# Half of the streamed weight loads issued from GpSimd instead of SyncE, and the last three phases in blocks of their own, in a transformer layer on 8 cores

## The chip, the cores and the metric

The kernel runs on the 8 cores of one Trainium2 chip. The sequence of 8192 tokens is split: each core computes 1024 output rows and recomputes what it needs of the 1024 rows before them, so no core waits for another. Every core reads the weights whole. The metric is the device time in microseconds (us) of the slowest core.

## The reference

```python
x = x + attn(layernorm(x))          # x: (1, 8192, 2048)
x = x + ffn(layernorm(x))
# attn: qkv = h @ Wqkv; q, k = rmsnorm over 2048; 16 heads of 128; rope;
#       scores where 0 <= q_idx - k_idx <= 1023; softmax; o @ Wo
# ffn:  x_q = 0.5 * sign of x beyond +-0.33, else 0
#       w = (0.6 * sign of weight beyond +-0.2, else 0) + rram_variation
#       y = einsum('bsd,od->bso', x_q, w)
```

All weights are float32 in HBM: Wqkv is 2048 x 6144, Wo, weight and rram_variation are 2048 x 2048. The products are made in bfloat16.

## The kernel before, in words

The program is written out by hand. A `Plan` collects one list of instructions per engine. Each engine works through its own list in order; waits on semaphores are entries of the same list, so whatever stands behind a wait on an engine waits too. The DMAs are issued by two engines: SyncE (SP) issues the loads of activations and weights, GpSimd (POOL) the other transfers. `Plan.run` (lines 127 to 134) writes the lists out as a block; at the end of a block all engines meet.

The blocks, by the names in the code:

- P0 and P1 load constants and normalize the core's 16 tiles of 128 rows; xlnT holds them transposed.
- P2k, P3q and P4v are the three projections. Each calls `qkv_pass` (line 360) for 4 chunks of 512 output columns. A chunk is first built: for d = 0 to 15, a 128 x 512 float32 piece of the weight (256 KB) is loaded into a staging buffer, wstgA for even d and wstgB for odd d (called A and B here), and VectorE (DVE) casts it into `wchunk` (line 383). Load d + 2 waits for the cast of piece d, since it overwrites the same staging buffer (line 378). Then TensorE (PE) waits for the last cast (line 386) and multiplies all 16 pieces for each row tile (line 394; 16 row tiles for k and v, 8 for q); ScalarE (ACT) moves each result out of PSUM (line 403). DVE begins the next chunk's casts when the last matmul of this chunk is done (line 373). There is only one `wchunk`, so PE has nothing to do while a chunk is built.
- In P4v, each evacuated v tile is spilled to HBM by a DMA of POOL (vhbm, lines 526 to 531), 16 spills per chunk.
- P5attn is the attention. It loads no weights.
- The last block, P8ffn, holds three phases. Output projection (lines 682 to 732): 128 transposes of the attention output, then 4 chunks of Wo, built as above with casts on line 705, matmuls on line 720 and the residual add on line 727. The residual piece of x_all comes by a DMA of POOL, one for each row tile and chunk, 4 buffers deep (lines 711 to 714). The first chunk is built while PE still transposes. Second layernorm and quantization (lines 737 to 785). FFN (lines 788 to 850): 4 chunks, and for each piece two loads, W (wfT) and R (rrT). ACT applies Sign to W twice (lines 811, 813), DVE adds the two (line 817) and then combines them with R into `wchunk` (line 822). There are two slots of buffers: slot 0 is wstgA and wstgB, slot 1 the two halves of ropeo. The loads of a slot wait for line 822 of its last use. After the build come the matmuls (line 835), the last sum on DVE (line 843), and the store of y by POOL, 8 per chunk (line 848).

Where the next chunk's first loads have a free buffer, SP issues them while PE still multiplies the chunk before.

```python
            for d in range(16):
                si = d % 2
                stg = wstgA if si == 0 else wstgB
                if stg_guard[si] is not None:
                    pl.wait("sync", cv, stg_guard[si])
                ld = pl.dma("sync", stg[:], ..., WS[si])
                pl.wait("vector", WS[si], ld)
```

Of the kernel before, what the change touches and what calls it, by code (L numbers as in the profile page):

```python
# [136 lines left out]
def build_nc(kphases=99, p1lvl=4):  # L137
    nc = bass.Bass("TRN2", target_bir_lowering=False)
# [3 lines left out]
    wo_d = nc.dram_tensor("wo", [D, D], F32, kind="ExternalInput").ap()  # L142
    wfT_d = nc.dram_tensor("wfT", [D, D], F32, kind="ExternalInput").ap()
    rrT_d = nc.dram_tensor("rrT", [D, D], F32, kind="ExternalInput").ap()
# [75 lines left out]
    WS = [Ctr(nc, "wA"), Ctr(nc, "wB"), Ctr(nc, "wC"), Ctr(nc, "wD")]  # L220
    dC = Ctr(nc, "dC")
    SP = [Ctr(nc, "spA"), Ctr(nc, "spB")]
    RNG = Ctr(nc, "rng")
    XR = [Ctr(nc, "xr0"), Ctr(nc, "xr1"), Ctr(nc, "xr2"), Ctr(nc, "xr3")]
    dO = Ctr(nc, "dO")
    ct = Ctr(nc, "ct")
    cv = Ctr(nc, "cv")
    cs = Ctr(nc, "cs")
    OWN = {"vector": cv, "scalar": cs}
# [25 lines left out]
    p = Plan(nc, OWN)  # L255
# [44 lines left out]
    p = Plan(nc, OWN)  # L300
# [59 lines left out]
    def qkv_pass(pl, col0, nchunks, tiles, dst_fn, pre_evac=None, post_evac=None,  # L360
                 w_dram=None, lhs_col=None):
        if w_dram is None:
            w_dram = wqkv_d
        if lhs_col is None:
            lhs_col = lambda t, d: 128 * (16 * t + d)
        ev = {}
        stg_guard = [None, None]
        par_guard = [None, None]
        prev_mm = None
        for ci in range(nchunks):  # L370
            c0 = col0 + 512 * ci
            if prev_mm is not None:
                pl.wait("vector", ct, prev_mm)
            for d in range(16):
                si = d % 2
                stg = wstgA if si == 0 else wstgB
                if stg_guard[si] is not None:
                    pl.wait("sync", cv, stg_guard[si])
                ld = pl.dma("sync", stg[:], w_dram[128 * d:128 * (d + 1), c0:c0 + 512],
                            WS[si])  # L380
                pl.wait("vector", WS[si], ld)
                dstw = wchunk[:, 512 * d:512 * (d + 1)]
                stg_guard[si] = pl.op("vector", lambda e, s=stg, w=dstw: e.tensor_copy(  # L383
                    out=w, in_=s), ins=[stg[:]], out=dstw, sem=cv)
            cast15 = stg_guard[1]
            pl.wait("tensor", cv, cast15)
            for ti, t in enumerate(tiles):
                par = ti % 2
                ps = (psA if par == 0 else psB)[:, 0:512]
                if par_guard[par] is not None:  # L390
                    pl.wait("tensor", cs, par_guard[par])
                ctm = None
                for d in range(16):
                    ctm = pl.op("tensor", lambda e, d=d, t=t, ps=ps: e.matmul(  # L394
                        ps, xlnT[:, lhs_col(t, d):lhs_col(t, d) + 128],
                        wchunk[:, 512 * d:512 * (d + 1)],
                        start=(d == 0), stop=(d == 15)),
                        sem=(ct if d == 15 else None))
                pl.wait("scalar", ct, ctm)
                if pre_evac is not None:  # L400
                    pre_evac(pl, t, ci)
                dst = dst_fn(t, ci)
                ev[(t, ci)] = pl.op("scalar", lambda e, ps=ps, dd=dst: e.copy(dd, ps),  # L403
                                    ins=[ps], out=dst, sem=cs)
                par_guard[par] = ev[(t, ci)]
                if post_evac is not None:
                    post_evac(pl, t, ci, ev[(t, ci)])
            prev_mm = ctm
        return ev
# [77 lines left out]
    p = Plan(nc, OWN)  # L487
# [12 lines left out]
    p = Plan(nc, OWN)  # L500
# [192 lines left out]
    for ci in range(4):  # L693
        c0 = 512 * ci
        if prev_mm6 is not None:
            p.wait("vector", ct, prev_mm6)
        for d in range(16):
            si = d % 2
            stg = wstgA if si == 0 else wstgB
            if stg_guard6[si] is not None:  # L700
                p.wait("sync", cv, stg_guard6[si])
            ld = p.dma("sync", stg[:], wo_d[128 * d:128 * (d + 1), c0:c0 + 512], WS[si])
            p.wait("vector", WS[si], ld)
            dstw = wchunk[:, 512 * d:512 * (d + 1)]
            stg_guard6[si] = p.op("vector", lambda e, s=stg, w=dstw: e.tensor_copy(  # L705
                out=w, in_=s), ins=[stg[:]], out=dstw, sem=cv)
        p.wait("tensor", cv, stg_guard6[1])
        for j in range(NQ):
            si = j % 4
            ps = (psA if j % 2 == 0 else psB)[:, 0:512]  # L710
            if xres_guard[si] is not None:
                p.wait("gpsimd", cv, xres_guard[si])
            xl = p.dma("gpsimd", xres[:, 512 * si:512 * (si + 1)],
                       x_d[128 * (8 + j):128 * (9 + j), c0:c0 + 512], XR[si])
            if par_guard6[j % 2] is not None:
                p.wait("tensor", cv, par_guard6[j % 2])
            ctm = None
            for h in range(NH):
                c0o = o_sb_base + 2048 * j + 128 * h
                ctm = p.op("tensor", lambda e, ps=ps, c0o=c0o, h=h: e.matmul(  # L720
                    ps, R1[:, c0o:c0o + 128], wchunk[:, 512 * h:512 * (h + 1)],
                    start=(h == 0), stop=(h == NH - 1)),
                    sem=(ct if h == NH - 1 else None))
            p.wait("vector", ct, ctm)
            p.wait("vector", XR[si], xl)
            dstx = x2[:, 2048 * j + c0:2048 * j + c0 + 512]
            evj = p.op("vector", lambda e, ps=ps, si=si, dd=dstx: e.tensor_add(
                dd, ps, xres[:, 512 * si:512 * (si + 1)]),
                ins=[ps, xres[:, 512 * si:512 * (si + 1)]], out=dstx, sem=cv)
            xres_guard[si] = evj  # L730
            par_guard6[j % 2] = evj
        prev_mm6 = ctm

    x2done = cv.v
    p.wait("scalar", cv, x2done)
    p.wait("vector", cv, x2done)
    th_of = lambda j: thr[:, 2 * j:2 * j + 1]
    tl_of = lambda j: thr[:, 2 * j + 1:2 * j + 2]
    tr7 = tr6
    cvx_prev = None  # L740
    for j in range(NQ):
        xt = x2[:, 2048 * j:2048 * (j + 1)]
# [40 lines left out]
            c0 = 2048 * j + 128 * d  # L783
            tr7.do(p, xqT[:, c0:c0 + 128], xqT[:, c0:c0 + 128], scale=0.5)
    cs_xqT = cs.v
    cvx_last = cvx_prev

    tmpA = [PTb[:, 0:512], PTb[:, 1024:1536]]
    tmpB = [PTb[:, 512:1024], PTb[:, 1536:2048]]
    stgW = [wstgA, ro2stgA[:, 0:512]]  # L790
    stgR = [wstgB, ro2stgA[:, 512:1024]]
    out_guard = None
    built_guard = [stg_guard6[1], max(stg_guard6[1] or 0, cvx_last or 0)]
    p.wait("scalar", cv, cvx_last)
    par_guard8 = [par_guard6[0], par_guard6[1]]
    prev_mm8 = None
    for ci in range(4):
        c0 = 512 * ci
# [1 line left out]
            p.wait("vector", ct, prev_mm8)  # L800
        for d in range(16):
            si = d % 2
            if built_guard[si] is not None:
                p.wait("sync", cv, built_guard[si])
                p.wait("scalar", cv, built_guard[si])
            ldw = p.dma("sync", stgW[si][:], wfT_d[128 * d:128 * (d + 1), c0:c0 + 512],
                        WS[si])
            ldr = p.dma("sync", stgR[si][:], rrT_d[128 * d:128 * (d + 1), c0:c0 + 512],
                        WS[2 + si])
            p.wait("scalar", WS[si], ldw)  # L810
            p.op("scalar", lambda e, s=stgW[si], tA=tmpA[si]: e.activation(  # L811
                out=tA, in_=s[:], func=AF.Sign, bias=-0.2), ins=[stgW[si][:]], out=tmpA[si])
            sgn = p.op("scalar", lambda e, s=stgW[si], tB=tmpB[si]: e.activation(  # L813
                out=tB, in_=s[:], func=AF.Sign, bias=0.2), ins=[stgW[si][:]], out=tmpB[si],
                sem=cs)
            p.wait("vector", cs, sgn)
            p.op("vector", lambda e, tA=tmpA[si], tB=tmpB[si]: e.tensor_add(tA, tA, tB),
                 ins=[tmpA[si], tmpB[si]], out=tmpA[si])
            p.wait("vector", WS[2 + si], ldr)
            dstw = wchunk[:, 512 * d:512 * (d + 1)]  # L820
            built_guard[si] = p.op(
                "vector", lambda e, s=stgR[si], w=dstw, tA=tmpA[si]: e.scalar_tensor_tensor(  # L822
                    w, s[:], 3.3333333, tA, ALU.mult, ALU.add),
                ins=[stgR[si][:], tmpA[si]], out=dstw, sem=cv)
# [23 lines left out]
            out_guard = p.dma("gpsimd", y_d[128 * j:128 * (j + 1), c0:c0 + 512],  # L848
                              outstg[:, 0:512], dO)
        prev_mm8 = ctm  # L850
    for cc in [dO, RNG, dC, SP[0], SP[1]] + XR:
        p.streams["gpsimd"].append(lambda e, s=cc.sem, v=cc.v: e.wait_ge(s, v))
    for cc in WS:
        p.streams["sync"].append(lambda e, s=cc.sem, v=cc.v: e.wait_ge(s, v))
# [54 lines left out]
```

## Time and profile before

| what | value |
|---|---|
| time, median of 2 runs | 3243.77 us (3237.33 to 3250.21) |
| profiled execution, its own time | 3240.53 us |
| its span on core 0, the slowest | 3238.5 us |
| spans of the 8 cores | 3218.8 to 3238.5 us |
| PE, ACT, DVE, POOL busy (share of the span) | 57%, 27%, 20%, 2% |
| P2k | about 270 to 884 us |
| P3q | about 884 to 1250 us |
| P4v | about 1250 to 1595 us |
| P5attn | about 1595 to 2502 us |
| output projection | about 2502 to 2767 us |
| second layernorm and quantization | about 2767 to 2903 us |
| FFN | about 2903 us to the end |

All times in the trace are microseconds from the span's start on core 0. The span leaves out 2.0 us of the execution's own time. A row of the timeline gives start, duration, engine, line and operation, and in square brackets how long the engine had been idle and what ended that. SPq is the queue of SyncE. Every DMA is issued from line 118, so loads are told apart by their buffers: wstgB<-wqkv is a load of Wqkv into buffer B.

### The profile page before, as it was taken

How to read it: one execution, taken by the hardware profiler on the slowest of the kernel's cores; microseconds unless marked ns; L12 is line 12 of the kernel's file. 1: busy time of each engine (PE TensorE's matmuls, PEld its weight loads, DVE VectorE, ACT ScalarE, POOL GpSimd, SP SyncE). 2: the span in 40 equal slices, each digit the busy share in tenths (PEclk: the TensorE clock that was granted, in tenths of full speed). 3: DMA queues.
4: the chain of work that ended last, by engine and by line, in shares of the span. 5: the costliest groups of instructions: out<-in, count | busy, mean ns of one | idle time of the engine just before them, and what ended most of it. 6: DMA issues, size and time to landing. Idle time of an engine off the chain costs nothing. (4 is left out here: it accounts for less than half of the span.)

```text
span 3238.5 us, 30548 instructions; the slowest of 8 cores (3218.8 to 3238.5 us)
## 1 busy us (share of the span) xinstructions
PE 1860.4 (57%) x9600; PEld 886.8 (27%) x9600; DVE 643.6 (20%) x1300; ACT 861.6 (27%) x1694; POOL 80.3 (2%) x153
## 2 busy tenths in 40 slices
PE   1223666503336423666898898889889735323333
PEld 0111322201112101232354454445445312101111
DVE  0001000033310032000203312330331121222222
ACT  4672111543301242111122222222123300442221
POOL 0000000000000000010100000000000000000000
PEclk9999888855568755888855555555555667656666
DMA  3211111000031102222200000000000233004333
GB/s 105 76 68 59 52 52 46 0 0 1 13 98 52 46 1 64 77 77 71 83 1 7 7 7 1 7 7 1 7 7 25 75 116 100 4 24 132 127 128 102
DMA packets 72828, 156.23 MB, mean 48 GB/s; under 512 B 12992, under 2 KB 12992, under 8 KB 70368
## 3 DMA queue, kind: packets, MB, share of 16 engines
q1 hardware_dynamic: 62016, 120.61, 11.6%
q0 software_dynamic: 10656, 33.67, 2.9%
q8 instruction: 81, 1.33, 0.2%
q14 instruction: 75, 0.61, 0.1%
HBM read 137.47 MB, written 16.78 MB: 48 GB/s over the span
## 5 line engine op out<-in xcount | busy, mean ns | idle before, releaser
L394 PE MATMUL psA<-wchunk,R 128*128 128x512 bf16 x1280 | 316.6, 404 | 326.8 <-DVE wchunk L383 326.8
L242 PE MATMUL psD<-identb,ropeo 128*128 128x128 bf16 x320 | 84.3, 264 | 488.0 <-DVE ropeo L478 254.8
L394 PE MATMUL psB<-wchunk,R 128*128 128x512 bf16 x1280 | 289.3, 379 | 0.0
L394 PEld LDWEIGHTS psA<-wchunk,R 128*128 128x128 bf16 x1280 | 130.7, 103 | 500.7 <-issue 368.2
L835 PE MATMUL psA<-wchunk,R 128*128 128x512 bf16 x256 | 65.5, 414 | 204.1 <-DVE wchunk L822 204.1
L242 PEld LDWEIGHTS psD<-identb,ropeo 128*128 128x128 bf16 x320 | 33.6, 105 | 539.6 <-issue 539.6
L615 PE MATMUL psA<-R 128*128 128x128 bf16 x576 | 163.5, 284 | 9.9 <-ACT wstgB L595 9.9
L383 DVE CAST wchunk<-wstgA 128x512 bf16<-128x512 f32 x96 | 41.0, 427 | 634.1 <-PE psB L394 439.6
L394 PEld LDWEIGHTS psB<-wchunk,R 128*128 128x128 bf16 x1280 | 125.3, 98 | 151.0
L615 PE MATMUL psB<-R 128*128 128x128 bf16 x576 | 163.7, 284 | 0.0
L246 ACT COPY R<-psD 128x128 bf16<-128x128 bf16 x384 | 101.8, 265 | 216.5 <-PE psC L242 123.6
L649 PE MATMUL psC<-R,PTb 128*128 128x128 bf16 x1152 | 145.6, 311 | 12.5 <-ACT R L666 12.5
L633 DVE TENSOR_TENSOR PTb<-PTb,masksb 128x128 bf16<-128x128 bf16 x128 | 28.8, 225 | 609.3 <-ACT PTb L628 609.3
L628 ACT ACTIVATE PTb<-psA 128x1152 bf16<-128x1152 f32 x64 | 72.3, 1130 | 183.3 <-PE psA L620 183.3
L649 PEld LDWEIGHTS psC<-R,PTb 128*128 128x128 bf16 x1152 | 112.1, 141 | 26.9 <-issue 12.9
L720 PE MATMUL psA<-wchunk,R 128*128 128x512 bf16 x256 | 66.4, 419 | 89.8 <-DVE wchunk L705 89.2
L628 ACT ACTIVATE PTb<-psB 128x1152 bf16<-128x1152 f32 x64 | 72.3, 1130 | 168.6 <-PE psB L620 168.6
L246 ACT COPY R<-psC 128x128 bf16<-128x128 bf16 x384 | 101.8, 265 | 37.8 <-PE psC L242 4.7
L403 ACT CAST R<-psA 128x512 bf16<-128x512 f32 x48 | 28.1, 585 | 305.4 <-PE psA L394 305.4
L573 DVE TENSOR_REDUCE nmaxs<-psA 128x1 f32<-128x1152 f32 x64 | 86.9, 1357 | 78.0 <-PE psA L569 72.2
L242 PE MATMUL psC<-identb,ropeo 128*128 128x128 bf16 x320 | 84.6, 264 | 27.2 <-ACT R L246 4.1
L242 PE MATMUL psD<-identb,R 128*128 128x128 bf16 x128 | 33.9, 265 | 113.8 <-DVE R L778 85.0
(112 smaller groups left out, 2268.6 us busy)
## 6 DMA issues: line engine op xcount, KB each, us to landing
wstgA<-wqkv SPq DMA_DIRECT2D x96, 256.0 KB, 2.7
wstgB<-wqkv SPq DMA_DIRECT2D x96, 256.0 KB, 2.8
wchunk<-x_all SPq DMA_DIRECT2D x16, 1024.0 KB, 4.7
vhbm<-PTb POOLq DMA_DIRECT2D x64, 128.0 KB, 2.1
R<-vhbm POOLq DMA_DIRECT2D x16, 512.0 KB, 4.1
wstgA<-wo SPq DMA_DIRECT2D x32, 256.0 KB, 2.9
wstgB<-wo SPq DMA_DIRECT2D x32, 256.0 KB, 3.0
R<-x_all POOLq DMA_DIRECT2D x32, 256.0 KB, 2.9
```

Of the source, the lines that this page charges most:

```text
L242: tv = pl.op("tensor", lambda e, s=slot, x=src_ap: e.transpose(s, x, identb[:]), sem=ct)
L246: g = pl.op("scalar", lambda e, s=slot, dd=dst_ap: e.copy(dd, s), ins=[slot], out=dst_ap, sem=cs)
L383: stg_guard[si] = pl.op("vector", lambda e, s=stg, w=dstw: e.tensor_copy(out=w, in_=s), ins=[stg[:]], out=dstw, sem=cv)
L394: ctm = pl.op("tensor", lambda e, d=d, t=t, ps=ps: e.matmul(ps, xlnT[:, lhs_col(t, d):lhs_col(t, d) + 128], wchunk[:, 512 * d:512 * (d + 1 ...
L403: ev[(t, ci)] = pl.op("scalar", lambda e, ps=ps, dd=dst: e.copy(dd, ps), ins=[ps], out=dst, sem=cs)
L573: red[h] = p.op("vector", lambda e, ps=ps, h=h: e.tensor_reduce(out=nmaxs[:, h:h + 1], in_=ps[:, 0:1152], axis=AX.X, op=ALU.max, negate=Tr ...
L615: p.op("tensor", lambda e, ps=ps, l=l, kb=kbase, q=q_ap: e.matmul(ps[:, 128 * l:128 * (l + 1)], kT[:, kb + 128 * l:kb + 128 * (l + 1)], q, ...
L628: expv = p.op("scalar", lambda e, ps=ps, PT=PT: e.activation(out=PT, in_=ps[:, 0:1152], func=AF.Exp), ins=[ps[:, 0:1152]], out=PT, sem=cs)
L633: p.op("vector", lambda e, PT=PT: e.tensor_mul(PT[:, 0:128], PT[:, 0:128], masks[:, 0:128]), ins=[PT[:, 0:128]], out=PT[:, 0:128])
L649: p.op("tensor", lambda e, PT=PT, l=l, sl=sl, h=h: e.matmul(psC[:, 0:128], PT[:, 128 * l:128 * (l + 1)], vring[:, 2048 * sl + 128 * h:2048 ...
L720: ctm = p.op("tensor", lambda e, ps=ps, c0o=c0o, h=h: e.matmul(ps, R1[:, c0o:c0o + 128], wchunk[:, 512 * h:512 * (h + 1)], start=(h == 0), ...
L835: ctm = p.op("tensor", lambda e, ps=ps, c0x=c0x, d=d: e.matmul(ps, xqT[:, c0x:c0x + 128], wchunk[:, 512 * d:512 * (d + 1)], start=(d == 0) ...
```

## The change

The pieces of odd d are loaded by POOL, on a new semaphore, instead of by SP, in `qkv_pass` and in the output projection. In the FFN every R load goes to POOL, in both slots, and POOL gets the wait for the slot. The last block is cut in three: P6wo, P7ln2 and P8ffn, each in a Plan of its own. So all engines meet at two more places, and no load of the FFN is issued before the second layernorm's block has ended. The waits that ordered the phases inside the one block are gone.

```diff
@@ qkv_pass
+                qeng = "sync" if si == 0 else "gpsimd"
+                qsem = WS[0] if si == 0 else WG0
                 if stg_guard[si] is not None:
-                    pl.wait("sync", cv, stg_guard[si])
-                ld = pl.dma("sync", stg[:], w_dram[128 * d:128 * (d + 1), c0:c0 + 512],
-                            WS[si])
-                pl.wait("vector", WS[si], ld)
+                    pl.wait(qeng, cv, stg_guard[si])
+                ld = pl.dma(qeng, stg[:], w_dram[128 * d:128 * (d + 1), c0:c0 + 512],
+                            qsem)
+                pl.wait("vector", qsem, ld)
@@ output projection
+            qeng = "sync" if si == 0 else "gpsimd"
+            qsem = WS[0] if si == 0 else WG0
             if stg_guard6[si] is not None:
-                p.wait("sync", cv, stg_guard6[si])
-            ld = p.dma("sync", stg[:], wo_d[128 * d:128 * (d + 1), c0:c0 + 512], WS[si])
-            p.wait("vector", WS[si], ld)
+                p.wait(qeng, cv, stg_guard6[si])
+            ld = p.dma(qeng, stg[:], wo_d[128 * d:128 * (d + 1), c0:c0 + 512], qsem)
+            p.wait("vector", qsem, ld)
@@ before the second layernorm
-    x2done = cv.v
-    p.wait("scalar", cv, x2done)
-    p.wait("vector", cv, x2done)
+    p.run("P6wo")
...
+    p = Plan(nc, OWN)
-    tr7 = tr6
+    tr7 = TrPipe()
@@ before the FFN
-    cvx_last = cvx_prev
-
+    p.run("P7ln2")
...
+    p = Plan(nc, OWN)
-    built_guard = [stg_guard6[1], max(stg_guard6[1] or 0, cvx_last or 0)]
-    p.wait("scalar", cv, cvx_last)
-    par_guard8 = [par_guard6[0], par_guard6[1]]
+    built_guard = [None, None]
+    par_guard8 = [None, None]
@@ FFN
+            rsem = WG0 if si == 0 else WG1
             if built_guard[si] is not None:
                 p.wait("sync", cv, built_guard[si])
+                p.wait("gpsimd", cv, built_guard[si])
                 p.wait("scalar", cv, built_guard[si])
-            ldr = p.dma("sync", stgR[si][:], rrT_d[128 * d:128 * (d + 1), c0:c0 + 512],
-                        WS[2 + si])
+            ldr = p.dma("gpsimd", stgR[si][:], rrT_d[128 * d:128 * (d + 1), c0:c0 + 512],
+                        rsem)
-            p.wait("vector", WS[2 + si], ldr)
+            p.wait("vector", rsem, ldr)
```

POOL's list around P4v, before (the rows of the spills, and the start of P5attn behind them):

```order
L134 UNCONDITIONAL_BRANCH [waits barrier_Pool_Activation_PE_DVE_SP_gather]
L118 DMA vhbm<-PTb 128x512 [waits cs] x64
L130 UNCONDITIONAL_BRANCH
L134 UNCONDITIONAL_BRANCH [waits barrier_Pool_Activation_PE_DVE_SP_gather]
L118 DMA R<-vhbm 128x2048 [waits spA,spB]
```

and the same place now:

```order
L118 DMA wstgB<-wqkv 128x512
L118 DMA wstgB<-wqkv 128x512 [waits cv] x7
L118 DMA vhbm<-PTb 128x512 [waits cs] x16
L118 DMA wstgB<-wqkv 128x512 [waits cv] x8
L118 DMA vhbm<-PTb 128x512 [waits cs] x16
L118 DMA wstgB<-wqkv 128x512 [waits cv] x8
L118 DMA vhbm<-PTb 128x512 [waits cs] x16
L118 DMA wstgB<-wqkv 128x512 [waits cv] x8
L118 DMA vhbm<-PTb 128x512 [waits cs] x16
```

The first B load of chunks 1 to 3 now stands behind the 16 spills of the chunk before.

POOL's list at the end of the program, before (residual loads, stores of y, and the waits of the end):

```order
L130 UNCONDITIONAL_BRANCH
L134 UNCONDITIONAL_BRANCH [waits barrier_Pool_Activation_PE_DVE_SP_gather]
L118 DMA R<-x_all 128x512 x4
L118 DMA R<-x_all 128x512 [waits cv] x28
L118 DMA y<-sa 128x512 [waits cv] x32
L130 UNCONDITIONAL_BRANCH [waits dO,rng,dC,spA,spB,xr0,xr1,xr2,xr3]
```

and now, from the end of the FFN's first build into its second:

```order
L118 DMA wstgB<-rrT 128x512 [waits cv]
L118 DMA ropeo<-rrT 128x512 [waits cv]
L118 DMA y<-sa 128x512 [waits cv] x8
L118 DMA wstgB<-rrT 128x512 [waits cv]
L118 DMA ropeo<-rrT 128x512 [waits cv]
L118 DMA wstgB<-rrT 128x512 [waits cv]
```

The first R loads of chunks 1 to 3 now stand behind the 8 stores of the chunk before.

SP's list inside an FFN build, before (two slots, W and R of each):

```order
L118 DMA wstgA<-wfT 128x512 [waits cv]
L118 DMA wstgB<-rrT 128x512
L118 DMA ropeo<-wfT 128x512 [waits cv]
L118 DMA ropeo<-rrT 128x512
L118 DMA wstgA<-wfT 128x512 [waits cv]
L118 DMA wstgB<-rrT 128x512
```

and now, from the start of its block:

```order
L134 UNCONDITIONAL_BRANCH [waits barrier_Pool_Activation_PE_DVE_SP_release]
L118 DMA wstgA<-wfT 128x512
L118 DMA ropeo<-wfT 128x512
L118 DMA wstgA<-wfT 128x512 [waits cv]
L118 DMA ropeo<-wfT 128x512 [waits cv]
L118 DMA wstgA<-wfT 128x512 [waits cv]
```

SP keeps the W loads alone, and the first two of them stand behind a meeting of all engines.

## Rows read from the trace of the kernel before

**Rows 1.** Waits, whole span: engine line <- waited for: us in total, times, longest.
```profile
PE psA L394 <- DVE wchunk L383: 326.8, 12, 30.4
DVE wchunk L383 <- DMA wstgA<-wqkv: 194.5, 87, 12.5
PE psA L835 <- DVE wchunk L822: 204.1, 4, 52.0
PE psA L720 <- DVE wchunk L705: 89.2, 3, 32.0
```

**Rows 2.** Timeline, K stage, one round: start, us, engine line, [idle before <-releaser].
```profile
533.44 0.43 DVE L383 CAST wchunk<-wstgA 128x512 bf16<-128x512 f32 x1 [2.60 <-DMA wstgA<-wqkv]
533.94 0.33 SPq L118 DMA_DIRECT2D wstgA<-wqkv  x1
534.08 0.43 DVE L383 CAST wchunk<-wstgB 128x512 bf16<-128x512 f32 x1 [0.21 <-DMA wstgB<-wqkv]
```

**Rows 3.** Timeline, K stage, first and last B cast of chunk 0.
```profile
274.39 0.43 DVE L383 CAST wchunk<-wstgB 128x512 bf16<-128x512 f32 x1 [0.28 <-DMA wstgB<-wqkv]
299.41 0.43 DVE L383 CAST wchunk<-wstgB 128x512 bf16<-128x512 f32 x1 [1.63 <-DMA wstgB<-wqkv]
```

**Rows 4.** DMA issues, 270 to 580 us: queue, count, size, median us to landing.
```profile
wstgA<-wqkv SPq DMA_DIRECT2D x32, 256.0 KB, 2.7
wstgB<-wqkv SPq DMA_DIRECT2D x32, 256.0 KB, 2.9
```

**Rows 5.** x_all loads from POOL, 2560 to 2760 us, all 28 of them.
```profile
L118 POOL DMA_DIRECT2D R<-x_all x28: 536/536/545, 2564.5 to 2753.4; - x28
DMA to landing us min/median/max: 2.8/2.9/4.3
```

**Rows 6.** Timeline, output projection: release of a POOL load, and its start.
```profile
2621.00 0.69 DVE L727 TENSOR_TENSOR R<-psA,R 128x512 f32<-128x512 f32 x1 [6.88 <-PE psA L720]
2622.25 0.54 POOL L118 DMA_DIRECT2D R<-x_all  x1 [33.01 <-DVE R L727]
```

**Rows 7.** Timeline, output projection, start of chunk 1's build.
```profile
2588.70 0.54 POOL L118 DMA_DIRECT2D R<-x_all  x1 [2.92 <-DVE wchunk L705]
2589.08 0.33 SPq L118 DMA_DIRECT2D wstgB<-wo  x1
2593.06 0.43 DVE L705 CAST wchunk<-wstgB 128x512 bf16<-128x512 f32 x1 [1.07 <-DMA wstgB<-wo]
```

**Rows 8.** Timeline, V stage, chunk 0 to chunk 1.
```profile
1336.42 0.43 DVE L383 CAST wchunk<-wstgB 128x512 bf16<-128x512 f32 x1
1336.97 0.54 POOL L118 DMA_DIRECT2D vhbm<-PTb  x1 [2.91 <-ACT PTb L403]
```

**Rows 9.** Timeline, FFN, chunk 0 to chunk 1.
```profile
2985.75 0.69 DVE L822 SCALAR_TENSOR_TENSOR wchunk<-wstgB,PTb 128x512 bf16<-128x512 f32 x1
2985.83 0.54 POOL L118 DMA_DIRECT2D y<-sa  x1 [3.22 <-DVE PTb L817]
```

**Rows 10.** Timeline, FFN: issue of an R load, and the step that reads it.
```profile
2912.79 0.43 SPq L118 DMA_DIRECT2D wstgB<-rrT  x1
...
2917.89 0.69 DVE L822 SCALAR_TENSOR_TENSOR wchunk<-wstgB,PTb 128x512 bf16<-128x512 f32 x1
```

**Rows 11.** DMA issues, whole span: W loads of the FFN, slots 0 and 1.
```profile
wstgA<-wfT SPq DMA_DIRECT2D x32, 256.0 KB, 3.0
ropeo<-wfT SPq DMA_DIRECT2D x32, 256.0 KB, 3.3
```

**Rows 12.** Timeline: the join of P1 and P2k.
```profile
270.26 0.27 ACT L246 COPY R<-psC 128x128 bf16<-128x128 bf16 x1 [0.15 <-PE psC L242]
270.78 0.33 SPq L118 DMA_DIRECT2D wstgA<-wqkv  x1
```

**Rows 13.** Timeline, PE: first two output tiles after a build.
```profile
299.98 6.53 PE L394 MATMUL psA<-wchunk,R 128*128 128x512 bf16 x16 [29.87 <-DVE wchunk L383]
306.34 3.62 PE L394 MATMUL psB<-wchunk,R 128*128 128x512 bf16 x16
```

More of the change, by code:

```diff
@@ L225, in build_nc @@
     dO = Ctr(nc, "dO")
+    WG0 = Ctr(nc, "wG0")
+    WG1 = Ctr(nc, "wG1")
     ct = Ctr(nc, "ct")
@@ L732, in build_nc @@
         prev_mm6 = ctm
-    x2done = cv.v
-    p.wait("scalar", cv, x2done)
-    p.wait("vector", cv, x2done)
+    p.run("P6wo")
+    if kphases < 7:
+        return _finish_early()
+    p = Plan(nc, OWN)
     th_of = lambda j: thr[:, 2 * j:2 * j + 1]
     tl_of = lambda j: thr[:, 2 * j + 1:2 * j + 2]
-    tr7 = tr6
+    tr7 = TrPipe()
     cvx_prev = None
@@ L785, in build_nc @@
     cs_xqT = cs.v
-    cvx_last = cvx_prev
+    p.run("P7ln2")
+    if kphases < 8:
+        return _finish_early()
+    p = Plan(nc, OWN)
     tmpA = [PTb[:, 0:512], PTb[:, 1024:1536]]
@@ L850, in build_nc @@
         prev_mm8 = ctm
-    for cc in [dO, RNG, dC, SP[0], SP[1]] + XR:
+    for cc in [dO, RNG, dC, SP[0], SP[1], WG0, WG1] + XR:
         p.streams["gpsimd"].append(lambda e, s=cc.sem, v=cc.v: e.wait_ge(s, v))
```

## The prediction, made before the changed kernel ran

> **What bounds the kernel now.** I read the waits of the whole span first. No engine is full: PE is busy for 57% of the span. PE's largest waits on this change's code are for the last cast of a chunk: 326.8 us in 12 waits in the three projections, 89.2 us in 3 waits in the output projection (its first chunk is built beside the transposes), 204.1 us in 4 waits in the FFN [rows 1]. So 15 builds by casts and 4 FFN builds lie bare on the path that sets the end, and a microsecond more in any of them is a microsecond more in the span.
>
> Next I asked what paces a build. DVE needs 0.43 us for a cast and then stands still for the next load: 2.60 us before the A cast of a round [rows 2], 194.5 us in 87 waits for A alone [rows 1]. The two buffers form two rings of dependence: cast, issue, landing, cast. SP issues 0.07 us after the cast ends (533.44 + 0.43 to 533.94) [rows 2]; the median landing counts from the start of the issue and is 2.7 us for A, 2.9 us for B [rows 4]. From the first to the last B cast of a chunk pass 299.41 - 274.39 = 25.02 us in 7 rounds, 3.57 us each [rows 3]. Check: 0.43 + 0.07 + 2.9 leaves 0.17 us from landing to cast. DVE takes A and B strictly in turn, so the slower buffer paces both. SP is busy for 0.33 us of issue per load [rows 2]: two of them in 3.57 us, so its issuing is not what fills the round.
>
> **The change, part 1: odd loads on POOL, 15 bare builds.** What must be known is the round trip of B through POOL. The trace has the same transfer from POOL, 256 KB of x_all with 128 rows of 2 KB. The release of one ends at 2621.00 + 0.69 = 2621.69 and POOL's instruction starts at 2622.25, 0.56 us later [rows 6], against SP's 0.07. From its start it lands in 2.8 us at least, 2.9 in the median, 4.3 at most, over 28 of them [rows 5]. So the start alone costs 0.49 us a round. For the landing the ends are these. Below: 2.8, 0.1 less than B has now, so +0.39 us. Above: 3.6, halfway between POOL's median and its maximum, so +1.19 us. I take 3.05, near the median with 0.15 on top, because x_all's loads mostly run alone, while B shares the engines with A. When B is slow, A waits for its turn, its cast follows B's at once and A's next load starts together with B's: two transfers from two queues. Three at once show what sharing can cost: POOL at 2588.70 and SP just before it with A, and the B load issued at 2589.08 is cast only at 2593.06, 3.98 us later instead of about 3.1 [rows 7]. My value is a round of 3.57 + 0.49 + 0.15 = 4.21 us. 15 builds of 7 rounds are 105 rounds: 105 x 0.64 = +67 us, ends +41 and +125.
>
> The Trainium skill, page "DMA: Bandwidth & Descriptors", section "Issuing engines are not separate DMA queues", says that all issuing engines share the same DMA engines and that issuing from several saves only the sequencer's time to initiate. The trace agrees in that SP's issue is short beside the landing. The same page (section "Latency and other measured facts") gives a first byte after about 1 us for a POOL load and 0.6 us for an SP load; an estimate by that is +0.4 us a round, +42 us for this part, where the rows give +67.
>
> **Part 2: B loads behind POOL's other work.** In V, the spill of the last row tile starts at 1336.97, while the first B cast of the next chunk runs at 1336.42, from a load that SP had issued long before [rows 8]. Now that load stands behind the spill: start 1336.97 + 0.54 = 1337.51, + 2.9 + 0.17 = 1340.6, so 4.2 us late. Three chunks follow another: +12.5 us (ends +12 and +13). In K and Q, POOL has nothing else, and the first loads stay hidden under the matmuls. In the output projection the residual loads in front wait only for tiles four back, so the first B loads stay hidden too; the first four residual loads of a chunk come behind the build's last B load and have 6.5 us of the first output tile [rows 13] besides; no cost. There is a small gain: they no longer collide with the start of the build, 0.9 us in [rows 7]. For 3 chunks I take -2 us (ends -3 and 0).
>
> In the FFN the first R load of a chunk stands behind the eighth store. The store starts at 2985.83 and the step that needs R ran at 2985.75 [rows 9]. Now: 2985.83 + 0.54 + 2.9 + 0.17 = 2989.4, 3.7 us late, and the slots' next loads wait for that step. Three chunks: +11 us (ends +10 and +12).
>
> **Part 3: R on POOL inside the FFN builds.** R is issued at 2912.79 and used at 2917.89, 5.1 us later [rows 10]. POOL would start it 0.56 us after the slot is free; SP does so after its 0.07 and W's issue of 0.33 us, so the start moves by about 0.2 us. With a landing of 3.6 us it is hidden, more than 1 us to spare. What sets the round there is W: landing, two Signs, two DVE steps. W's landings are 3.0 and 3.3 us in the slots [rows 11], against A's 2.7. Without R in SP's queue they may fall to 2.7-3.0; with R beside them from another queue they may rise by half a microsecond, as B did in [rows 7]. 4 builds of 7 rounds: 28 x (-0.3 to +0.5) = -8 to +14; I take +0.1, +3 us, since the bytes are the same.
>
> **Part 4: blocks of their own.** A meeting of all engines costs little: 270.26 + 0.27 = 270.53 to SP's next issue at 270.78, 0.25 us [rows 12]. Two new ones: 0.5 us. But the FFN's first loads can't be issued in P7 any more: 2.9 + 0.17 us bare. Together +3.6 us (ends +3 and +5). The removed waits were met long before and give nothing.
>
> PE's pace: the first output tile after a build takes 6.53 us and the next 3.62 [rows 13]. That price is paid at each build already, after 29.87 us without matmuls, and I see no reason for it to grow at 34 us.
>
> **Sum**, on the profiled execution's own 3240.5 us: 67 + 12.5 - 2 + 11 + 3 + 3.6 = +95, so 3336. The median of the runs shown is 3.3 us higher, so I forecast 3339 us, 2.9% slower. Adding all low ends gives 41 + 12 - 3 + 10 - 8 + 3 = +55, 3299; all high ends +169, 3413.
>
> **Rivals.**
> (a) Not slower: SP's one queue is what holds the loads up. Place: the rings of A, B and the FFN's W. If the turnaround of B on POOL, from cast end to landing, were below 2.95 us, A's own ring would pace the build: 0.43 + 0.07 + 2.7 + 0.17 = 3.37 us a round, 105 x -0.20 = -21 us; W would land in 2.7: 28 x -0.4 = -11; the other terms +25. Together -7, 3237 us. For it: B lands later than A, and the FFN's W later still [rows 4, 11]. Against it: 0.56 + 2.8 = 3.36 us is the least that the trace shows for POOL [rows 5, 6].
> (b) Descriptors held up by DVE: the A cast that follows each B cast at once falls into the time in which POOL prepares the B load. If POOL had to wait for it, each round would grow by a cast more, 105 x 0.43 = +45 us: 3384 us. For it: nothing plain. Against it: POOL's load at 2588.70 was prepared during two casts and its instruction took the same 0.54 us [rows 6, 7]; its landing may hide something. The Trainium skill, page "SBUF — State Buffer", section "Who interferes with whom", says that casts can lock GpSimd out of a shared port, so that it can't write descriptors; the rows don't show it, and it is this rival's only real support.
> (c) The landing of B stays at 2.8 and W gains: all low ends, 3299 us, within 2%. It is the lower edge of the forecast.
>
> **Chances.** Forecast (with (c) as its edge) 0.68, (a) 0.13, (b) 0.14, 0.05 for what I don't see. The range from 3297 to 3395 us holds the forecast, its low end and (b), and leaves out (a) and sums near all high ends. A measurement of this kernel tells about 2%, here 65 us, so the line for slower is at 3309. Of the forecast's 0.68 some 0.09 lie below it; (a) lies within 2%, and only 0.03 of all is beyond 2% faster. So faster 0.03, same 0.22, slower 0.75.
>
> **What would show it.** Right: POOL's B issue starts 0.5 to 0.6 us after the B cast; DVE's long wait in a round is before the B cast, and A's cast follows at once by the end of a chunk; B casts 4.0 to 4.4 us apart; PE's wait in front of each projection chunk 4 to 5 us longer, and 4 more in V's chunks 1 to 3; the first FFN step of chunks 1 to 3 some 3.7 us late. Wrong: B casts 3.4 us apart (rival a), or POOL landings above 3.4 us while the issue starts on time (rival b, or more sharing than I took); W landings in the FFN away from 3.0 to 3.4; or a first output tile much slower than 6.5 us.

## The result and the profile after

| | before | after |
|---|---|---|
| time, median | 3249.82 us (10 runs) | 3402.0 us (11 runs) |
| ratio, after to before | | 1.0478, 95% interval 1.0447 to 1.0510 |
| profiled execution, span of the slowest core | 3238.5 us | 3412.7 us |
| spans of the 8 cores | 3218.8 to 3238.5 us | 3354.1 to 3412.7 us |

The change makes the kernel 4.8% slower, 152 us by the medians. The forecast was slower by 2.9%, 3339 us, with 3395 us as its upper end. The sign was right, the size was not: the result lies outside the range.

The same waits as [rows 1], in the changed kernel (its lines are 4 to 11 higher):

```profile
PE psA L398 <- DVE wchunk L387: 445.4, 12, 42.1
DVE wchunk L387 <- DMA wstgB<-wqkv: 294.8, 90, 5.3
PE psA L846 <- DVE wchunk L833: 224.9, 4, 58.5
PE psA L726 <- DVE wchunk L711: 103.9, 3, 35.9
DVE wchunk L387 <- DMA wstgA<-wqkv: 80.4, 41, 12.3
```

PE's waits for the last cast grow by 445.4 - 326.8 = 118.6 us in the projections, by 14.7 us in the output projection and by 20.8 us in the FFN: 154 of the 174 us by which the slowest core's span grew. In the projections DVE used to wait mostly for A; now B has 294.8 us of its waits, where it had 65.4.

The first build of the K stage, DVE alone (start, duration, operation, idle time before it):

```profile
278.22 0.43 DVE L387 CAST wchunk<-wstgB 128x512 bf16<-128x512 f32 x1 [1.45 <-DMA wstgB<-wqkv]
279.69 0.43 DVE L387 CAST wchunk<-wstgA 128x512 bf16<-128x512 f32 x1 [1.04 <-DMA wstgA<-wqkv]
282.39 0.43 DVE L387 CAST wchunk<-wstgB 128x512 bf16<-128x512 f32 x1 [2.27 <-DMA wstgB<-wqkv]
...
291.16 0.43 DVE L387 CAST wchunk<-wstgB 128x512 bf16<-128x512 f32 x1 [3.15 <-DMA wstgB<-wqkv]
291.77 0.43 DVE L387 CAST wchunk<-wstgA 128x512 bf16<-128x512 f32 x1 [0.18 <-DMA wstgA<-wqkv]
296.23 0.43 DVE L387 CAST wchunk<-wstgB 128x512 bf16<-128x512 f32 x1 [4.04 <-DMA wstgB<-wqkv]
296.76 0.43 DVE L387 CAST wchunk<-wstgA 128x512 bf16<-128x512 f32 x1
301.32 0.43 DVE L387 CAST wchunk<-wstgB 128x512 bf16<-128x512 f32 x1 [4.13 <-DMA wstgB<-wqkv]
```

Two kinds of rounds are to be seen. Early on, B casts are 4.17 us apart (278.22 to 282.39) and A is cast somewhere between. Later they are 5.07 and 5.09 us apart, and A's cast follows B's at once, with no idle time: A had landed and was waiting for its turn. Once that is so, A's next load starts right beside B's. The issues, early (276 to 289 us) and late (291.5 to 303 us), last column the median us to landing:

```profile
wstgA<-wqkv SPq DMA_DIRECT2D x4, 256.0 KB, 3.3
wstgB<-wqkv POOLq DMA_DIRECT2D x3, 256.0 KB, 3.0
...
wstgB<-wqkv POOLq DMA_DIRECT2D x3, 256.0 KB, 3.9
wstgA<-wqkv SPq DMA_DIRECT2D x3, 256.0 KB, 3.2
```

B lands 3.0 us after its issue in the early rounds and 3.9 us in the late ones. What the late rounds have in common is two things at once: A's load starts together with B's, and A's cast runs on DVE just before POOL's instruction for B begins. An early round and a late one, the two issues:

```profile
279.20 0.54 POOL L118 DMA_DIRECT2D wstgB<-wqkv  x1 [3.52 <-DVE wchunk L387]
280.19 0.33 SPq L118 DMA_DIRECT2D wstgA<-wqkv  x1
...
297.22 0.54 POOL L118 DMA_DIRECT2D wstgB<-wqkv  x1 [4.54 <-DVE wchunk L387]
297.26 5.42 SPq L118 DMA_DIRECT2D wstgA<-wqkv  x2
```

(The last row holds two issues; the first starts at 297.26.)

The start of a V build, chunk 1, where [rows 8] stood:

```profile
1405.28 0.43 DVE L387 CAST wchunk<-wstgA 128x512 bf16<-128x512 f32 x1 [57.73 <-PE psB L398]
1405.78 6.16 SPq L118 DMA_DIRECT2D wstgA<-wqkv  x2
1406.36 0.54 POOL L118 DMA_DIRECT2D vhbm<-PTb  x1 [2.92 <-ACT PTb L407]
1406.89 0.54 POOL L118 DMA_DIRECT2D wstgB<-wqkv  x1
1410.58 0.43 DVE L387 CAST wchunk<-wstgB 128x512 bf16<-128x512 f32 x1 [4.87 <-DMA wstgB<-wqkv]
1411.11 0.43 DVE L387 CAST wchunk<-wstgA 128x512 bf16<-128x512 f32 x1
1411.58 0.54 POOL L118 DMA_DIRECT2D wstgB<-wqkv  x1 [4.15 <-DVE wchunk L387]
1415.71 0.43 DVE L387 CAST wchunk<-wstgB 128x512 bf16<-128x512 f32 x1 [4.18 <-DMA wstgB<-wqkv]
```

The B load stands behind the spill, as forecast. DVE stands idle for 4.87 us before the cast of B, and A has landed meanwhile, so the pair is side by side from the very first round (1410.58 to 1415.71 is 5.13 us). Builds from first to last cast, summed over four chunks of a stage: K 102.6 to 131.5 us, Q 101.8 to 137.7, V 101.5 to 155.6; the three bare builds of Wo 84.2 to 99.0, the four of the FFN 184.8 to 180.9 (read off the casts' starts in the timeline).

The start of the FFN's second build, where [rows 9] stood:

```profile
3129.11 0.54 POOL L118 DMA_DIRECT2D y<-sa  x1 [4.42 <-DVE PTb L828]
3129.65 0.54 POOL L118 DMA_DIRECT2D wstgB<-rrT  x1
3130.18 0.54 POOL L118 DMA_DIRECT2D ropeo<-rrT  x1
3134.59 0.69 DVE L833 SCALAR_TENSOR_TENSOR wchunk<-wstgB,PTb 128x512 bf16<-128x512 f32 x1 [5.70 <-DMA wstgB<-rrT]
```

The step that needs R starts 5.5 us after the store's issue; in the kernel before it ran 0.1 us ahead of it. In the third and fourth builds it starts 6.5 and 5.1 us after.

### The profile page after: what moved, and what is told of

It is laid out like the page before. It is cut to its first block and busy times, and to the rows that moved or that the text cites. A ratio compares the mean times of both kernels' runs of the same rounds, so it can differ in the third digit from the quotient of the medians.

```text
span 3412.7 us, 30625 instructions; the slowest of 8 cores (3354.1 to 3412.7 us)
## 1 busy us (share of the span) xinstructions
PE 1862.6 (55%) x9600; PEld 886.3 (26%) x9600; DVE 643.8 (19%) x1300; ACT 865.3 (25%) x1696; POOL 183.7 (5%) x345
## 5 line engine op out<-in xcount | busy, mean ns | idle before, releaser
L398 PE MATMUL psA<-wchunk,R 128*128 128x512 bf16 x1280 | 312.7, 401 | 445.4 <-DVE wchunk L387 445.4
L118 POOL DMA_DIRECT2D wstgB<-wqkv x96 | 51.8, 540 | 1395.7 <-POOLq L130 769.9
```

The lines of the kernel that those rows point to most:

```text
L118: return self.op(eng, lambda e, d=dst, s=src: e.dma_start(out=d, in_=s), sem=ctr, n=16)
L398: ctm = pl.op("tensor", lambda e, d=d, t=t, ps=ps: e.matmul(ps, xlnT[:, lhs_col(t, d):lhs_col(t, d) + 128], wchunk[:, 512 * d:512 * (d + 1 ...
```

## The experiments

Theories for the 0.9 us that B loses in the late rounds. S: the two transfers, started together, share what carries them. D: DVE's cast of A holds up POOL while it prepares B's load (rival b of the prediction). First, one run takes away A's transfers and keeps the casts, and one keeps the transfers and takes the casts away from DVE.

**A loaded once per chunk.**

```diff
+                if si == 1 or d == 0:
...
                     ld = pl.dma(qeng, stg[:], ..., qsem)
                     pl.wait("vector", qsem, ld)
```

> The changed kernel, but in the three projections buffer A is loaded only for d = 0 of each chunk and cast again for every even d: the weights of d = 2, 4, ... are left out, all casts and all B loads stay. B is then alone on the DMA engines, while A's cast still follows B's at once. In the changed kernel the late rounds of a build take 5.1 us and B lands 3.9 us after its issue; the early ones take 4.15 us. Theory S (two transfers that run at once share the engines): B lands in 2.8 to 3.1 us, every round takes 4.0 to 4.2 us, a build 29 to 30 us from the first to the last cast. Theory D (the A cast on DVE holds up POOL's preparation of the B load): B lands in 3.4 to 3.9 us, all rounds 4.6 to 5.1 us, a build 33 to 36 us.

Measured: one run, 3364.58 us. The K stage's B loads, 270 to 580 us, and two rounds late in its first build:

```profile
wstgB<-wqkv POOLq DMA_DIRECT2D x31, 256.0 KB, 3.0
```

```profile
291.56 0.43 DVE L388 CAST wchunk<-wstgB 128x512 bf16<-128x512 f32 x1 [3.21 <-DMA wstgB<-wqkv]
292.09 0.43 DVE L388 CAST wchunk<-wstgA 128x512 bf16<-128x512 f32 x1
292.54 0.54 POOL L118 DMA_DIRECT2D wstgB<-wqkv  x1 [3.63 <-DVE wchunk L388]
295.68 0.43 DVE L388 CAST wchunk<-wstgB 128x512 bf16<-128x512 f32 x1 [3.16 <-DMA wstgB<-wqkv]
```

A's cast follows B's at once, as in the late rounds, and the round takes 4.12 us, not 5.1. All rounds of K and Q but each build's last take 4.1 to 4.6 us. The last ones take 4.7 to 5.2 us in six of the eight builds: there the A load for the next chunk starts beside B's. The builds took 30 to 31 us, 1 us over the expectation, for that last round. S stands.

How far D is refuted depends on when POOL prepares the load. In this run A's cast lies in the 0.55 us between the end of B's cast and the start of POOL's instruction (292.09 to 292.52, before 292.54), in 600 of the 672 B loads of all cores that no A load started beside; B landed in 3.0 us with it and without it. In the changed kernel 98 of the B loads that start apart from A have most of a cast between the start of POOL's instruction and the load's first packet, 1.24 us later; they landed in 3.0 us too, as did the 173 without. The cast lies inside the 0.54 us of the instruction only where A's load starts 0.5 to 0.75 us after B's. B landed in 3.4 us there (26 loads), and in 3.3 us at the same distance in the next run, where the cast is ACT's (36 loads). So some 0.1 to 0.2 us at most could be the cast's in these few, and not the 0.9 us.

**A cast by ACT.**

```diff
+                    pl.wait("scalar", qsem, ld)
+                    if stg_guard[1] is not None:
+                        pl.wait("scalar", cv, stg_guard[1])
+                    stg_guard[0] = pl.op("scalar", lambda e, s=stg, w=dstw: e.copy(
+                        w, s[:]), ins=[stg[:]], out=dstw, sem=cs)
...
+                    pl.wait("vector", cs, stg_guard[0])
```

> The changed kernel, but in the three projections the A casts are made by ACT, each waiting for the B cast before it, and each B cast waits for the A cast before it, so that the order is kept and DVE does nothing while POOL prepares a B load. Theory S (sharing): B still lands in about 3.9 us once A's load starts beside it, late rounds 5.0 to 5.3 us. Theory D (DVE's cast holds up POOL): B lands in 3.0 to 3.4 us and late rounds take 4.2 to 4.6 us.

Measured: one run, 3426.36 us. The late rounds of K and Q take mostly 4.8 to 5.1 us, against mostly 4.8 to 5.2 in the changed kernel; the first four of a build 4.2 to 4.9. In V's chunk 1 (1416 to 1450 us), where all rounds are of the late kind, the loads land like this:

```profile
wstgB<-wqkv POOLq DMA_DIRECT2D x8, 256.0 KB, 3.6
wstgA<-wqkv SPq DMA_DIRECT2D x6, 256.0 KB, 3.7
```

Neither expectation was met to the letter: B is at 3.6 us, below the 3.9 of S and above the 3.4 of D, and A has gone from 3.3 to 3.7. The rounds lie above D's and for the most part just below S's. So most of the 0.9 us stays when DVE casts nothing beside POOL's load, and a slower A beside a faster B is what two transfers that share would show: ACT's cast takes 0.62 us, so A's load starts about 0.3 us after B's here.

**The parts of the change.** Three kernels take one part each. The cut of the last block alone:

> The kernel before with the last block cut in three and nothing else. From the rows of the changed kernel: two meetings of all engines 0.5 us, the first FFN loads bare 3 us, and two activation table loads of 1.28 us that appear at the start of the new blocks, 2.6 us: +6 us in all (ratio 1.002). Rival: the cut also explains that each store of y lands 0.4 us later in the changed kernel (2.8 us instead of 2.4); then the FFN grows by 12 us more and the whole is +18 us (1.0055).

Measured: ratio 1.0018, interval 0.9982 to 1.0055, +6 us by its middle, though the interval also holds none. The profiles say where it is: from the end of the last residual add to the first operation of the second layernorm 1.5 us more than before, and from the last evacuation of that block to the first step of the FFN's build 7.3 us where it was 1.9. Stores of y land in 2.4 us as before. The activation table load at the new block's start is there:

```profile
2769.36 1.28 ACT L747 ACT_TABLE_LOAD   x1 [205.48 <-PEq L130]
```

R on POOL alone (the load, its wait and its semaphore, nothing cut):

> The kernel before with only the FFN's R loads moved to POOL. If the first R load of a chunk behind the last store of y is the only cost, 3 chunk starts of 5.5 us as in the changed kernel: +16 us (1.005). If the R loads on POOL's queue also make each store of y slower (2.8 us to land instead of 2.4), 32 stores in a row on the path add 12 us: +28 us (1.009). If the builds gain by W alone in SP's queue (0.2 us a round, 28 rounds) it is 6 us less in either case.

Measured: ratio 1.0048, interval 1.0012 to 1.0085, +16 us. Stores land in 2.4 us on core 0. The middle is the first case; the second, +28 us (1.009), lies just outside the interval. That the builds neither gain nor lose is not told by it (185.2 us for the four, 184.8 before).

B on POOL alone:

> The kernel before with only the odd loads of the projections and of the output projection on POOL. If the parts add up, it is the changed kernel less the cut (+6 us measured) and less R on POOL (+16 us measured): 155 - 22 = +133 us (ratio 1.041), with the builds of the three projections 39 us longer in V and 26 to 31 us longer in K and in Q. Rival: the parts help each other (a POOL queue that also carries R slows more than its share), then clearly less than +133 us here, +110 us (1.034) or below.

Measured: ratio 1.0456, interval 1.0390 to 1.0522, +148 us. The expected +133 us lies within the interval, near its lower end; the rival of +110 us does not. K, Q and V builds sum to 132.1, 131.6 and 155.0 us, as in the changed kernel within 6 us. So nearly all of the loss is this part's. The three bare builds of Wo took 104.1 us in this trace, 5 us more than in the changed kernel's.

**Is it POOL, or is it two transfers that start together?** First B from ACT's queue, whose start is as quick as SP's.

```diff
+                qeng = "sync" if si == 0 else "scalar"
+                qsem = WS[0] if si == 0 else WG0
```

> The kernel before with the odd loads of the three projections issued from ACT's queue; the output projection and the FFN stay as before. Theory S (a second queue is no trouble in itself; POOL's later start makes B the slower ring, so that A and B end up side by side): B rounds stay at 3.4 to 3.8 us, landings 2.7 to 3.0 us, builds 25 to 26.5 us. Rival theory Q (two queues on the same DMA engines slow each other): B lands in 3.3 us or more, rounds 4.0 us or more, builds 29 us or more. In both the first B load of chunks 1 to 3 stands behind ACT's last evacuation, 3 to 3.7 us late, 9 times, +30 us: S gives 1.010, Q 1.020 or more.

Measured: ratio 1.0033, interval 0.9988 to 1.0077: no difference that can be told. Start of a build in K, chunk 1:

```profile
358.17 14.27 ACTq L118 DMA_DIRECT2D wstgB<-wqkv  x5
358.69 14.57 SPq L118 DMA_DIRECT2D wstgA<-wqkv  x5
361.13 0.43 DVE L387 CAST wchunk<-wstgB 128x512 bf16<-128x512 f32 x1 [2.51 <-DMA wstgB<-wqkv]
361.72 0.43 DVE L387 CAST wchunk<-wstgA 128x512 bf16<-128x512 f32 x1 [0.16 <-DVE wchunk L387]
364.57 0.43 DVE L387 CAST wchunk<-wstgB 128x512 bf16<-128x512 f32 x1 [2.43 <-DMA wstgB<-wqkv]
```

Rounds of 3.44 us, builds 25.7 to 28.0 us, landings 2.8 and 2.9 us: two queues are no trouble in themselves. The same bytes move as before and sooner than in the changed kernel, so it isn't the amount of traffic either. The expected +30 us for late first loads came in small: the pair turns round instead (B is cast just before A of the next round), and the builds of chunks 1 to 3 grow by 0.4 to 2.8 us, all twelve together by 15 us in this trace. Here A and B mostly start 0.5 to 0.6 us apart. In 24 pairs of this run, over all cores, they started within 0.05 us of each other; those landed in 3.4 us (A) and 3.7 us (B). The next kernel makes them start together every time; its one edit against this one:

```diff
                 if stg_guard[si] is not None:
-                    pl.wait(qeng, cv, stg_guard[si])
+                    pl.wait(qeng, cv, stg_guard[0])
```

> The kernel with B issued from ACT's queue, but each B load now waits for the A cast as well, so that A on SP and B on ACT start at the same moment in every round, as A on SP and B on POOL do in the late rounds of the changed kernel (there A lands in 3.3 us and B in 3.9 us). Theory S1 (two transfers that start together slow each other, whatever issues them): the two land in 3.3 to 3.9 us. Theory S2 (it takes a POOL load beside an SP load): both land in 2.7 to 3.1 us.

Measured: one run, 3400.77 us, beside 3242.27 us of the kernel before. A round in K, chunk 1, on core 6:

```profile
380.59 5.35 SPq L118 DMA_DIRECT2D wstgA<-wqkv  x2
380.59 5.39 ACTq L118 DMA_DIRECT2D wstgB<-wqkv  x2
384.58 0.43 DVE L387 CAST wchunk<-wstgB 128x512 bf16<-128x512 f32 x1 [4.07 <-DMA wstgB<-wqkv]
```

The DMA issues of the same run, 270 to 600 us, last column the median us to landing:

```profile
wstgA<-wqkv SPq DMA_DIRECT2D x32, 256.0 KB, 3.5
wstgB<-wqkv ACTq DMA_DIRECT2D x31, 256.0 KB, 3.8
```

S1 holds. With no POOL in it, the two land in 3.5 and 3.8 us when they start in the same instant, and the round takes mostly 4.9 to 5.1 us. Of the 1.5 us over the round of 3.44 us, some 0.5 are the wait that the edit adds (B's load now waits for A's cast too), and 0.9 the slower landing. With ACT and SP, half a microsecond between the starts is enough for 2.8 and 2.9.

**Both loads on POOL.**

> The kernel before with both loads, A and B, of the three projections issued from POOL (the output projection stays on SP). The two then stand in one queue, half a microsecond apart. Theory S1: they land in 2.9 to 3.2 us as alone, rounds take 4.0 to 4.3 us, a build 29 to 31 us, shorter than the 32 to 34 us of the changed kernel's half and half. If POOL's loads are slow beside any other load, one of the two lands in 3.5 us or more and a build takes 33 us or more.

Measured: one run, 3330.3 us, beside 3242.27 us of the kernel before: +88 us. Landings 3.1 us (A) and 3.2 us (B), builds 30.2 to 31.9 us, rounds 4.0 to 4.8. In one queue the two can't start together:

```profile
365.24 0.54 POOL L118 DMA_DIRECT2D wstgA<-wqkv  x1 [57.73 <-DVE wchunk L387]
365.77 0.54 POOL L118 DMA_DIRECT2D wstgB<-wqkv  x1
368.78 0.43 DVE L387 CAST wchunk<-wstgA 128x512 bf16<-128x512 f32 x1 [3.56 <-DMA wstgA<-wqkv]
```

Moving all the projections' loads to POOL costs less than moving half of them: their twelve builds grow by 69 us here, by 113 us in the kernel with B alone on POOL (whose +148 us holds the output projection too).

**More loads in flight.** If the round trip of a buffer is the pace, more buffers are the cure. ropeo is idle during all these builds and holds two more.

```diff
-                si = d % 2
-                stg = wstgA if si == 0 else wstgB
+                si = d % 4
+                stg = [wstgA, wstgB, ro2stgA[:, 0:512], ro2stgA[:, 512:1024]][si]
```

> The kernel before with four staging buffers instead of two in the projections and the output projection (the two halves of ropeo, which is idle there), all loads on SP. If a build is paced by the round trip of a buffer, four in flight halve it until the transfers themselves fill the time: two at once took 0.9 us more than one, so 16 loads take 13 to 15 us, a build 15 to 17 us instead of 25, 15 builds, -130 us (ratio 0.96). Rival: the pace is set by the DMA engines or HBM with all 8 cores loading the same weights; then a build stays above 22 us and the ratio above 0.985.

Measured: ratio 0.9524, interval 0.9497 to 0.9551, 3098.16 us: faster than both kernels. PE's waits in the projections and in the output projection:

```profile
PE psA L394 <- DVE wchunk L383: 217.3, 12, 22.8
...
PE psA L720 <- DVE wchunk L705: 59.4, 3, 21.4
```

They fall by 109.5 and 29.8 us, 139 together. Builds take 14.9 to 18.0 us in the projections and, bare, 17.0 to 19.9 in the output projection. A round of four takes mostly 4.0 to 4.8 us in K and Q (the first of a chunk up to 7.7 us in V and the output projection), 1 MB in it, while a single load lands in 3.5 to 3.9 us (the output projection's in 3.9 to 4.4): now the transfers themselves have a share in the pace.

The same four buffers with the odd loads on POOL:

> The same four buffers with the odd loads on POOL. If the half microsecond of POOL's start is the cost, depth hides it: builds 16 to 18 us in K and Q, and only the first loads behind the spills in V remain (3 x 4 us): ratio to the kernel before 0.965 to 0.975. If a POOL load costs more the more is in flight, builds are 20 us or longer and the ratio is above 0.985.

Measured: ratio 0.9762, interval 0.9684 to 0.9840. K and Q builds take 17.2 to 19.9 us, V's chunks 1 to 3 23.3 to 24.6 us. The middle falls short of the expected 0.965 to 0.975, and the interval holds its upper part. Depth hides about half of POOL's cost: 0.9762 against 0.9524 is some 77 us, where with two buffers it was 148. Rounds of four take mostly 4.9 to 5.7 us in K, 0.7 us and more over those on SP alone.

## Why the prediction failed, by its steps

- **What bounds the kernel** was right. Bare builds, paced by a buffer's round trip, carry the loss; the four-buffer kernel shows the same thing from the other side.
- **Part 1, POOL's start.** Right: 0.55 us from the B cast to POOL's instruction (278.22 + 0.43 = 278.65; the row at 279.20), where [rows 6] had 0.56. The early rounds take 4.1 to 4.2 us, against my 4.21.
- **Part 1, the landing, is the step that failed.** The term was 3.05 us with 3.6 us as the upper end, and the round of 4.21 us hung on it; measured were 3.0 us apart from A and 3.9 us beside A, with rounds of 5.1 us. I had named the mechanism (A is cast at once after B and starts with it), yet priced it as 0.15 us on the mean. Two things were mis-sized. First, its price: 0.9 us, shown with A's transfers taken away and with two quick queues started together. [Rows 7] had a load 3.98 us from issue to cast, and I did not let it set the upper end. Second, its share. B's ring is the slower one (4.15 us a round; A's casts came 3.2 to 4.2 us apart in the first build), and that closes the gap between the two by the fourth or fifth of seven rounds in most of K and Q, and earlier in some. Of core 0's 96 A loads 50 started within 0.2 us of a B load; I took the alone case for the rule. K and Q grew by 65 us in 56 rounds, 1.2 us each instead of 0.64.
- **Part 2, V.** The lateness was about right (4.2 us forecast; the B cast moved to 1410.58 from about 1405.8, 4.8 us). But I added it to unchanged rounds. The late B is what puts the pair side by side from round one: chunks 1 to 3 take 40 to 41 us, where K's take 32 to 34; 4.8 us of that is the lateness, the rest the rounds. V grew by 54 us; the forecast gave it 18 for its 28 rounds and 12.5 for the queue.
- **Part 2, output projection.** +14.8 us; the forecast had 13 for its 21 rounds less 2. Near, but B landed in 3.4 us here too, not 3.05, and with B alone on POOL the same builds grew by 19.9 us. The gain of 2 us wasn't tested; what cancels what is open.
- **Part 2, FFN.** 5.5, 6.5 and 5.1 us at the three chunk starts, not 3.7: the R load lands in 4.7, 5.8 and 4.4 us between the store ahead of it and the R load behind it on the queue. I used the landing of a load alone again.
- **Part 3.** W's landings hardly moved (3.0 and 3.2 us, from 3.0 and 3.3 [rows 11]). The builds became 3.9 us shorter; I had +3. R on POOL as a whole costs +16 us, against +14 in the forecast. That this is close is luck: in the changed kernel's trace the starts cost 17 us where I had 11, and the builds gave 4 back where I had 3 more.
- **Part 4.** +6 us measured, +3.6 forecast, within what can be told. I had missed the activation table load at the head of each new block that has ACT work, 1.28 us twice.
- **Rival (a)** is refuted: B never turned round in 2.95 us on POOL. **Rival (b)** named the right moment and the wrong cause. A's cast falls just before POOL's instruction, not into it, and neither there nor between the instruction and the first packet did a cast change the 3.0 us of the landing; with the casts of A on ACT most of the loss stayed. The rule of the Trainium skill, page "SBUF — State Buffer", section "Who interferes with whom", that casts can lock GpSimd out of a shared port did not show in these runs: in this kernel the casts cost POOL's loads nothing that can be told. Only for the 26 loads with the cast inside POOL's instruction can 0.1 to 0.2 us not be ruled out. The other rule (page "DMA: Bandwidth & Descriptors", section "Issuing engines are not separate DMA queues") agrees with the runs: B from ACT's queue brought no gain, ratio 1.0033.

By size: B on POOL cost 148 us where parts 1 and 2 together had 77 without the FFN; the three parts measured singly add up to 170 us, the whole is 155 by its ratio (145 to 166 by its interval), and the single intervals are 12 us and more to either side.

## What to carry to other kernels

When two buffers are read strictly in turn, making one of them slower also moves the other: it waits for its turn, and from then on both loads start together. Price such a change with the landing of two transfers started at once for every round after the gap between them has closed (from the first in V, from the fourth or fifth in most of K and Q), not with a landing alone. And where a build is paced by a buffer's round trip, give it more buffers before giving it another queue: two more made this kernel 4.8% faster, another queue left it as it was (ACT's, with B alone) or made it slower by as much (POOL's, with B and R).

## What the runs showed of the hardware

- Two loads of 256 KB from two queues, started in the same instant, landed in 3.5 and 3.8 us; 0.5 us apart, in 2.8 and 2.9 us. It doesn't take POOL, but the distance that is enough depends on it: in the changed kernel, over all cores, loads of A issued 0.5 to 0.75 us after B's still landed in 3.4 to 3.5 us, both of them, and only from 0.75 us on in 2.9 and 3.0. There the first packet comes 1.24 us after the start of POOL's instruction and 0.95 us after that of SP's.
- The packets in the traces show what the two share. With ACT and SP, 0.5 to 0.75 us apart (257 pairs), the packets of each load are spread over 1.4 to 1.5 us and those of the two together over 2.2 us. Started in the same instant (744 pairs) the two together need 2.4 us, hardly more, but each load's own are now spread over 2.0 to 2.1 us: both end late, instead of one early and one late. With POOL beside SP (282 pairs) it is B's first packet that comes late, 1.8 us after the issue instead of 1.24, and the two together again need 2.4 us. (All are medians.)
- In the two new blocks the first operation of ACT brought an activation table load of 1.28 us, even though the same phases inside one block had none at that place.
- In the profiled execution of the changed kernel the stores of y took 2.8 us to land on core 0, and 2.3 to 2.4 us on the seven other cores, as before. 32 of them lie on the path, so 0.4 us each is 13 us of this core's span. Neither the cut nor R on POOL brings it on core 0 (2.4 us in both; with R on POOL core 2 shows 2.7). It differs from run to run and core to core; its cause is open.
